# Rows of destinations selected as three bfloat16 parts, and the identity of the diagonals in PSUM

## What is computed

```python
norm = jnp.sqrt(jnp.sum(h * h, axis=-1, keepdims=True))
nh = h / jnp.maximum(norm, EPS)
cos = jnp.sum(nh[src] * nh[dst], axis=-1)
e = beta * cos
m = jax.ops.segment_max(e, dst, num_segments=n_nodes)
ee = jnp.exp(e - m[dst])
den = jax.ops.segment_sum(ee, dst, num_segments=n_nodes)
p = ee / den[dst]
out = jax.ops.segment_sum(h[src] * p[:, None], dst, num_segments=n_nodes)
return jax.nn.relu(out)
```

## Time and profile before

| | |
|---|---|
| three runs | 13307.4, 13310.5 and 13315.4 us, median 13310.5 |
| span of the profiled execution | 13318.3 us (only its span is given) |
| PE busy | 7676.6 us (58%) |
| DVE busy | 5885.9 us (44%) |
| ACT busy | 2405.7 us (18%) |
| POOL busy | 9586.8 us (72%) |
| chain that ended last | POOL 56%, issue 19%, PE 13%, DVE 6%, DMA 5% |

### The profile page before, as it was taken

The page is one execution under the profiler, slowest core; times in us unless marked ns, Lnnn a source line. Parts: engine busy times, 40 slices in busy tenths (PEclk is TensorE's granted clock), DMA queues, the critical chain, the costliest instruction groups (busy, mean ns, idle before and its releaser), DMA issues.

```text
span 13318.3 us, 116975 instructions
## 1 busy us (share of the span) xinstructions
PE 7676.6 (58%) x34308; PEld 6050.5 (45%) x34308; DVE 5885.9 (44%) x12726; ACT 2405.7 (18%) x5360; POOL 9586.8 (72%) x9933
## 2 busy tenths in 40 slices
PE   8330001444444999999888888885555555444444
PEld 2220001333333777777666666663333333333333
DVE  6990001333333777777666666663222222212211
ACT  0000000000000444444444444441000000000000
POOL 5777776777776777777666666665777776777777
PEclk5555555555555555555555555555555555555555
DMA  1000001111112222222322222222222223111112
GB/s 36 5 15 10 5 5 41 27 27 27 27 27 26 52 52 52 52 53 55 48 54 53 54 53 53 53 52 38 50 49 50 50 49 52 27 27 27 27 27 26
DMA packets 430124, 505.70 MB, mean 38 GB/s; under 512 B 235856, under 2 KB 245584, under 8 KB 417584
## 3 DMA queue, kind: packets, MB, share of 16 engines
q0 software_dynamic: 317504, 279.59, 13.7%
q1 hardware_dynamic: 97730, 214.09, 4.7%
q10 hardware_dynamic: 14316, 4.81, 0.2%
HBM read 397.49 MB, written 94.54 MB: 37 GB/s over the span
## 4 chain that ended last, share of the span: by engine, by line
POOL 56%; issue 19%; PE 13%; DVE 6%; DMA 5%; ACT 1%; DVEq 0%; SPq 0%; POOLq 0%
POOL Z L653 44%; POOL bins_dst L629 12%; PE ps L1511 5%; PE ps L1478 3%; DMA Z<-table,pd 2%; DMA Z<-table_a,pd 2%; DVE pay_d L1174 1%; PE ps L1545 1%; PE ps L1485 1%; PE ps L1487 1%; PE ps L1502 1%; DVE Z L1097 1%; ACT L719 0%; PE ps L1497 0%; DVE Z L1166 0%
## 5 line engine op out<-in xcount | busy, mean ns | idle before, releaser
L653 POOL DMA_INDIRECT Z<-table,pd x4986 | 4866.1, 976 | 1975.6 <-issue 1461.9
L1527 PE MATMUL ps<-Z 128*128 128x65 f32 x9972 | 2341.8, 422 | 3346.3 <-DVE Z L1166 1200.9
L1527 PEld LDWEIGHTS ps<-Z 128*128 128x128 f32 x9972 | 2185.3, 329 | 3682.0 <-DVE Z L1166 1310.0
L1100 DVE TENSOR_TENSOR Z<-ps,pd 128x768 f32<-128x768 f32 x831 | 794.7, 957 | 2863.4 <-PE ps L1527 2855.3
L653 POOL DMA_INDIRECT Z<-table_a,pd x1662 | 1569.6, 944 | 605.7 <-issue 492.6
L629 POOL DMA_INDIRECT bins_dst<-slot_d x1612 | 1578.5, 979 | 589.3 <-issue 489.4
L653 POOL DMA_INDIRECT Z<-table_b,pd x1662 | 1569.3, 944 | 549.3 <-issue 506.4
L1478 PEld LDWEIGHTS ps<-pay_d,Z 128*128 128x128 f32 x6648 | 1538.2, 333 | 124.4 <-issue 124.4
L1511 PE MATMUL ps<-Z 128*128 128x65 f32 x6648 | 1564.0, 422 | 3.1 <-DVE Z L1166 3.0
L1511 PEld LDWEIGHTS ps<-Z 128*128 128x128 f32 x6648 | 1459.6, 329 | 189.8 <-issue 185.0
L1478 PE MATMUL ps<-pay_d,Z 128*128 x6648 | 1474.5, 412 | 24.4 <-ACT Z L705 24.4
(11 more groups left out here) (238 smaller groups left out, 8089.8 us busy)
## 6 DMA issues: line engine op xcount, KB each, us to landing
pay_d<-locals_ SPq DMA_DIRECT2D x92, 1152.0 KB
Z<-table,pd POOLq DMA_INDIRECT x4986, 2.5
table_b<-pay_d SPq DMA_DIRECT2D x192, 256.0 KB, 2.4
Z<-table_a,pd POOLq DMA_INDIRECT x1662, 2.5
Z<-table_b,pd POOLq DMA_INDIRECT x1662, 2.4
bins_dst<-slot_d POOLq DMA_INDIRECT x1612, 2.1
table_a<-kept SPq DMA_DIRECT2D x94, 256.0 KB, 2.1
slot_d<-pay_d SPq DMA_DIRECT2D x62, 91.0 KB, 1.9
```

The costliest lines, as they stand in the source:

```text
L653: nc.gpsimd.indirect_dma_start(rows[:, at.slot, j, 0:width], None, ps_.table, bass.IndirectOffsetOnAxis(ap=pdi[:, g * ITEMS + j, ps_.colum ...
L1100: v.tensor_tensor(hot_d[:, at.three, :, :], every, nodes, ALU.is_equal).then_inc(hot_f_made, 1)
L1527: last = mm(p_pair[:, at.three, bass.ds(offset_of(at, j), ROW)], hot_d[:, at.three, j, :], given, start=False, stop=j == ITEMS - 1)
```

## The change

The unit rows are kept as three bfloat16 parts (the row rounded, the rest rounded, what is left), two of them in the place of the float32 rows, one in `Z` where the wide one-hots were. For each item PE adds up three bfloat16 matmuls with the narrow one-hots `hot_t` in place of one float32 matmul with the wide ones. ACT's step `wide_hots` and its semaphore go. DVE's `unit_row` has five operations for one, so passes 0 and 1 have 18 and 12 steps a block for 14 and 8. The identity that `diagonals` multiplies is read from PSUM, in float32, where it is copied once a softmax pass; before it was bfloat16 in SBUF.

```diff
-        hot_32 = Z[:, o:o + 2 * ITEMS * P].rearrange("p (s j e) -> p s j e", s=2, j=ITEMS)
+        unit_low = Z[:, o:o + (NB * ROW + 1) // 2].bitcast(BF16)
-        unit = pay_d[:, SPAN:2 * SPAN].bitcast(F32)
+        unit_parts = [pay_d[:, SPAN:2 * SPAN].bitcast(BF16)[:, k * SPAN:(k + 1) * SPAN] for k in range(2)] + [unit_low]
+        ident_ps = ps[:, 2, 2 * P:3 * P]
-        OPS, ROOTS = (14, 8, 15, 13, 3), (5, 2, 2, 2, 0)
+        OPS, ROOTS = (18, 12, 15, 13, 3), (5, 2, 2, 2, 0)
-                def wide_hots(at):
-                    act.wait_ge(dst_rows, done(e + at.g - 2))
-                    nc.scalar.activation(hot_32[:, at.two, :, :].rearrange("p j e -> p (j e)"), pen_t[:, at.slot, :], ACT.Relu,
-                                         bias=ones[:, 0:1], scale=-1.0 / BIG).then_inc(hot_32_made, 1)
+                if ps_.softmax:
+                    link(v.tensor_copy(ident_ps, ident[:, :]))
-                    v.tensor_tensor(diagonal[:, at.two, :, :], ident_b[:, :].unsqueeze(1).to_broadcast([P, ITEMS, P]),
+                    v.tensor_tensor(diagonal[:, at.two, :, :], ident_ps.unsqueeze(1).to_broadcast([P, ITEMS, P]),
                                     score[:, at.three, :].unsqueeze(2).to_broadcast([P, ITEMS, P]), ALU.mult).then_inc(scored_b, 1)
                 def unit_row(rank, k):
-                    to = unit[:, bass.ds(rank.place, D)]
-                    then(rank, k, v.tensor_scalar(to, tabs[:, rank.spare, 0:D], blk_c[:, 3:4], None, ALU.mult))
+                    to = [part[:, bass.ds(rank.place, D)] for part in unit_parts]
+                    then(rank, k, v.tensor_scalar(blk_h, tabs[:, rank.spare, 0:D], blk_c[:, 3:4], None, ALU.mult))
+                    then(rank, k + 1, v.tensor_scalar(to[0], blk_h, 1.0, None, ALU.mult))
+                    then(rank, k + 2, v.tensor_tensor(h_rest[:, :], blk_h, to[0], ALU.subtract))
+                    then(rank, k + 3, v.tensor_scalar(to[1], h_rest[:, :], 1.0, None, ALU.mult))
+                    then(rank, k + 4, v.tensor_tensor(to[2], h_rest[:, :], to[1], ALU.subtract))
...
-                    pe.wait_ge(hot_32_made, done(e + at.g))
+                    pe.wait_ge(hot_t_made, done(e + at.g))
                     for j in range(ITEMS):
                         place = (first_place(at) + offset_of(at, j)).with_bounds(min_val=0, max_val=(NB - 1) * ROW)
-                        of_block = unit[:, bass.ds(place, D)]
-                        last = mm(p_row[:, at.two, j, :], hot_32[:, at.two, j, :], of_block, start=True, stop=True)
+                        for k, part in enumerate(unit_parts):
+                            last = mm(p_row[:, at.two, j, :], hot_t[:, at.slot, j, :], part[:, bass.ds(place, D)],
+                                      start=k == 0, stop=k == 2)
```

More of the change, by code:

```diff
@@ L182, in gnn_program @@
         o = 2 * NB * D
-        hot_32 = Z[:, o:o + 2 * ITEMS * P].rearrange("p (s j e) -> p s j e", s=2, j=ITEMS)
+        hot_f = Z[:, o:o + 2 * ITEMS * P].rearrange("p (s j n) -> p s j n", s=2, j=ITEMS)
         o += 2 * ITEMS * P
-        hot_f = Z[:, o:o + 2 * ITEMS * P].rearrange("p (s j n) -> p s j n", s=2, j=ITEMS)
-        assert 4 * ITEMS * P <= NB * ROW
+        unit_low = Z[:, o:o + (NB * ROW + 1) // 2].bitcast(BF16)
+        assert 3 * ITEMS * ROW <= 2 * ITEMS * P and 2 * ITEMS * P + (NB * ROW + 1) // 2 <= NB * ROW
         pen_t = Z[:, NB * D:NB * D + RING * ITEMS * P // 2].bitcast(BF16).rearrange("p (s c) -> p s c", s=RING)
@@ L342, in gnn_program @@
         keys_made, keys_spread = sem("keys_made"), sem("keys_spread")
-        blk_steps = [sem(f"blk_step{k}") for k in range(1, 16)]
+        blk_steps = [sem(f"blk_step{k}") for k in range(1, 19)]
         blk_root = sem("blk_root")
@@ L353, in gnn_program @@
         local_loaded = [sem("local_loaded0"), sem("local_loaded1")]
-        hot_t_made, hot_32_made, pen_made, fallen = sem("hot_t_made"), sem("hot_32_made"), sem("pen_made"), sem("fallen")
+        hot_t_made, pen_made, fallen = sem("hot_t_made"), sem("pen_made"), sem("fallen")
         hot_f_made = sem("hot_f_made")
@@ L669, in _ @@
         def _(act):
-            for s in (hot_t_made, hot_32_made, pen_made, fallen, keep_made, exp_made):
+            for s in (hot_t_made, pen_made, fallen, keep_made, exp_made):
                 act.sem_inc(s, CREDIT + NG)
@@ L769, in work @@
                     steps += [(3, penalty), (3, narrow_hots), (-1, falls), (-1, factors), (-1, exponentials),
-                              (3, wide_hots), (-2 if p == 2 else -3, idle)]
+                              (-2 if p == 2 else -3, idle)]
                 steps += [(RING - 1, idle), (-2, idle)]
```

## The result

The changed kernel takes 13341.0 us, median of nine runs (13336.2 to 13352.8), against 13308.8 (13303.6 to 13315.4) for the kernel before: a ratio of 1.0024, 95% interval 1.0015 to 1.0032. It is 32 us slower, where 67 us faster was forecast, and outside the range. The profiled execution spans 13337.6 us.

What follows compares the result with a forecast made beforehand. GpSimd's gathers were taken to bound pass 1 and a loop through TensorE pass 2. Terms of -41, -32 and +6 made -67 us: 13251 from the profiled span, 13243 us as median, range 13150 to 13300.

Steps and rivals of the forecast that it cites:

- Identity in PSUM: Pass 1: gathers held up by the diagonals' two SBUF inputs return to pass 0's length, -41 us; landing waits stay.
- Rival E: Pass 1: the longer gathers have another cause, a landing or the broadcast's packets, and stay; 13284 us, chance 0.08.
- Unit rows: Passes 0 and 1: five linked operations for one, +1.0 us a block, covered in pass 1's rounds, +6 us in the drains.
- So some 1.5 stay: Pass 1: of VectorE's 3.5 us a round of waits for gathers, 1.5 us remain, covering the added operations.
- the pauses: Drains of passes 0 and 1: three uncovered blocks each before the tables are complete, +6 us in all.
- Rival D: Pass 1: VectorE becomes the limit and the added operations eat GpSimd's gain, +42 us; 13286 us, chance 0.10.
- Bfloat16 select: Pass 2: the clearing comes 0.19 us earlier in 168 turns with products, -32 us, bounds -8 and -123.
- rivals B: Pass 2: the array, not the sequencer, sets the pace; turns with products fall to 7.5 us; 13024 us, chance 0.06.
- C: Pass 2: bfloat16 raises TensorE's clock, L1511 saves 1.2 to 1.4 us, turns end at 7.5; near 13024, chance 0.03.
- A: Pass 2: sequencer slower, gap 0.12 us per bfloat16 address, clearing 0.71 us later in 168 turns; 13427 us, chance 0.10.
- the gap: Pass 2: sequencer's pause between address computations of bfloat16 matmuls, taken as 0.07 us; against the change from 0.089 on.
- The turn without a product, behind the block's sums: Pass 2: clearing moves 0.33 us back (4.00 to 4.33) in 42 turns, covered by 0.47 us, so nothing.

Runs made afterwards that it cites:

- e14: Kernel before with the identity in PSUM and nothing else (its added register reads vanished), on the result's kind of chip: 13277.1 us, 0.9975.
- e13: Kernel before with four more linked operations behind each unit row in passes 0 and 1, on the result's kind of chip: 13363.3 us, 1.0039.
- e10: Changed kernel with SP's load of local numbers ahead of the store in pass 1, on a 15.24 ms chip: 1.0029 to the kernel before.
- e17: Changed kernel with the store waiting for the table row's last step, not the unit row's, on a 15.24 ms chip: 1.0039 to the kernel before.
- e16: Kernel before with each load of local numbers in pass 1 waiting until the store has landed, on a 15.24 ms chip: 1.0015.
- e5: Changed kernel with the select's matmuls reading a fixed operand, so no address is computed, on a 15.33 ms chip: 1.0124 to the kernel before.
- e6: Changed kernel selecting two of the three bfloat16 parts, on a 15.33 ms chip: 1.0121 to the kernel before.
- e1: Kernel before with the identity in PSUM and nothing else, on a 15.24 ms chip: 0.9957, 70 us less.
- e11: Kernel before with the identity in PSUM and SP's load ahead of the store in pass 1, on a 15.24 ms chip: 0.9954.
- e18: Kernel before with the identity in PSUM and the load ahead of the store, as e11, on another chip: 0.9956.
- e8: Kernel before, unaltered, as reference on a 15.24 ms chip: 0.9996.
- e7: Changed kernel, unaltered, on a 15.33 ms chip: 1.0205 to the kernel before.
- e9: Changed kernel, unaltered, on a 15.24 ms chip: 1.0085 to the kernel before.

## Why the prediction was wrong

**Identity in PSUM: right.** The gathers are 0.944 us in the mean and none of pass 1 is over 0.97; -41 was forecast, -31 measured alone (e14), since 8 us went into waits for landings (54.4 for 46.6), which the prediction has staying as they are. Rival E is out.

**Unit rows: the step that failed.** "So some 1.5 stay", the prediction says of VectorE's waits in pass 1, and books 0 for 42 blocks and +6 for the pauses. The pauses came as forecast, +3.0 and +3.5. Pass 1 cost 42 us (e13). The cover on VectorE did exist: GpSimd waits 1.2 us for messages, and VectorE still waits 125 us for landings. What was missed is who else waits for the block's last step: SP, whose queue holds behind that store the load of 1152 KB. One us more of linked operations moves the load 1.05 us back, and the landings behind it too: 45 x 1.05 = 47 us, for 39 us of added waits in e13 and 54 after. e10, e17 and e16 show from three sides that the load's place moves the landings, all on the other chips. Rival D had the size (+42) by another mechanism, VectorE as the limit, which the waits refute.

**Bfloat16 select: the mechanism right, the size 0 for -32.** The sequencer paces it (e5, e6); rivals B and C are out, as is A (for C: L1515 still takes 2.82 us, at a granted clock of 0.50 in pass 2). From 7024.34 to 7027.03 its 18 computations take 2.70 us, of which 1.33 are their own (12 of 46 ns); 17 gaps of 0.081 are the rest. The term that was mis-sized is the gap: 0.07 was taken, and 0.078, the bound "as with four instructions", was nearly right. So handing over a bfloat16 matmul cost the sequencer as much as a float32 one. 18 gaps at 0.081 are 0.19 us more than at 0.07, the computations were 0.04 shorter than the 1.37 taken, and the second read of places 0.02 longer. Together they are 0.17 of the 0.19 us forecast. From the end of that read to L1506 it was 0.06 us, where 0.05 was taken. The turn without a product, behind the block's sums, went from 4.01 to 4.50 us between the two marks (4.33 forecast) and from 8.83 to 8.86 in length, covered as said.

**The sum** by what was measured on the result's kind of chip: -31 (e14) and +55 (e13) make +24. The other 8 us of the +32 no run takes apart: they may be the two together, or the select, of which pass 2 shows nothing (2518 us for 2516) and pass 1 was not measured alone. Moving SP's order or the store's wait in the changed kernel was not tried on such a chip either.

**The better version** is the identity alone: 0.9975 there, and 0.9957 (e1) on the others, where the gain has another source. With the load moved too it is 0.9954 (e11) and 0.9956 (e18), no more than without.

## What to carry to other kernels

Before booking linked operations as covered, list every queue that waits for the last of them, and what stands behind that wait in the queue: here a DMA of 1152 KB that had nothing to do with the block. Let a store wait for the step that makes its data, not for the last of a chain. And when an operand's address comes from a register, count the sequencer's time for each matmul: here 0.125 us where a constant is added (46 ns and a gap of 0.079) and up to 0.29 where the computation is long (211 ns and a gap). Cutting one float32 matmul into three bfloat16 ones bought nothing here, because each had its own address.

## What the runs showed of the hardware

The sequencer's gap between two address computations was 0.081 us in the mean with a bfloat16 matmul handed over in it (two instructions: the 18 have 18 weight loads and 18 matmuls in the turn of the trace after) and 0.078 us with a float32 one (four: the six have 12 and 12 before).

The computations of addresses (`ISA` in the orders of instructions, `FUSED_REGOPS` in the earlier trace rows) took the array no time before. While L1478 kept it busy, from 7009.17 to 7011.83, for 2.66 of 2.66 us, the sequencer made L1511's five, 51 to 171 ns each, from 7010.8 to 7011.7. In pass 1 L1478's matmuls start 0.213 us apart (median), in the 2095 cases with a computation beside them and in the 953 without.

With one input of the diagonals in PSUM the gathers are 0.944 us in the mean, and the diagonals take the same 0.96 us. The gathers of pass 1 took 1568.2 us in e14 against 1610.1 in the kernel before, and 1568 in e1 against 1681 in e8. In pass 1 of the kernel before, 97 of the 1662 gathers took over 1 us, up to 1.68, and each of them started 0.10 to 0.77 us into a diagonals operation. The 173 that met the reduction behind the diagonals (L1127) and not the diagonals took 0.95 us at most. The diagonals themselves took 0.957 to 1.034 us before and 0.956 to 0.959 after, so no trace here shows that VectorE is held up as the gathers are.

On the chips of 15.24 and 15.33 ms, VectorE often starts long after the recorded end of the matmuls that it waits for, and the profile writes "remote" for what released it. Pass 0 of e7:

```profile
3525.42 2.82 PE L1531 MATMUL ps<-Z 128*128 128x65 f32 x12 [0.61 <-issue]
3528.17 0.50 PE L1506 MATMUL ps<-zeros_b 1*128 1x390 bf16 x1
3548.43 0.96 DVE L1098 TENSOR_TENSOR Z<-ps,pd 128x768 f32<-128x768 f32 x1 [22.59 <-remote]
```

Nothing in the trace accounts for the 20 us. On the result's chips neither kernel has a wait of this kind in passes 0 to 2. On the others both have them: e8, the kernel before, 1620, 619 and 133 us in its passes 0, 1 and 2. In most turns with products of e1's pass 2 the sums still reach VectorE 0.28 us after their recorded end, as on the result's chips; in e5 they do so up to 7 us later.

The waits also show where the ratios of 1.0205 (e7) and 1.0085 (e9) part: in pass 2, e7 has 437 us of them and e9 142, and the pass takes 2825 and 2642 us. With the shorter select they grow, to 567 us in e6 and 687 in e5. What makes them stays open: no run tells it apart.
